# The router's matmuls on bf16 parts: eight small matmuls per tile of tokens in place of four in fp32r

## What is computed

```python
x = x + tanh(g_xattn[0]) * attention(layernorm(x), ctx, Wq, Wk, Wv, Wo, q_norm_w, k_norm_w, ...)
y = layernorm(x)
probs = softmax(y @ w_router, axis=-1)          # w_router: 256 x 8
top_v, top_i = top_k(probs, 2)
top_v = top_v / sum(top_v)
# two of eight experts per token, weighted by top_v, and a shared expert
x = x + tanh(g_ffn[0]) * (2.5 * routed + shared)
```

## Time and profile before

| | us |
|---|---|
| median of 3 runs (1231.79 to 1233.23) | 1233.18 |
| the profiled execution | 1232.97 |
| its span, first to last instruction | 1231.2 |
| granted TensorE clock, mean of the span | 0.998 of full speed |

### The profile page before, as it was taken

The page is one execution under the profiler, slowest core; times in us unless marked ns, Lnnn a source line. Parts: engine busy times, 40 slices in busy tenths (PEclk is TensorE's granted clock), DMA queues, the critical chain, the costliest instruction groups (busy, mean ns, idle before and its releaser), DMA issues.

```text
span 1231.2 us, 31490 instructions
## 1 busy us (share of the span) xinstructions
PE 1206.6 (98%) x8781; PEld 1137.8 (92%) x8782; DVE 1009.8 (82%) x2992; ACT 884.6 (72%) x3754; POOL 922.4 (75%) x1124
## 2 busy tenths in 40 slices
PE   6899999999999999999999999999999999999998
PEld 3788999999999999999999999999999899999997
DVE  8788888888888888888888888888888677777443
ACT  7978777777777777777777777777777546666322
POOL 2778888888888888888888888888887425555654
PEclk9999999999999999999999999999999999999999
DMA  6634233322222222223333333222236536554574
GB/s 179 198 116 130 73 109 104 100 90 90 90 90 90 94 90 94 90 90 96 115 107 98 103 108 118 90 75 75 75 110 214 191 108 185 168 156 148 187 232 155
DMA packets 128792, 148.57 MB, mean 121 GB/s; under 512 B 13824, under 2 KB 108288, under 8 KB 127968
## 3 DMA queue, kind: packets, MB, share of 16 engines
q1 hardware_dynamic: 122256, 130.16, 34.9%
q0 software_dynamic: 6480, 17.77, 3.9%
HBM read 66.93 MB, written 80.76 MB: 120 GB/s over the span
## 4 chain that ended last, share of the span: by engine, by line
PE 92%; DVE 3%; ACT 2%; DMA 1%; issue 1%; SPq 0%; another core or an unknown queue 0%; POOL 0%; DVEq 0%; POOLq 0%; ACTq 0%
PE b_kv L1711 14%; PE b_q L1697 14%; PE b_o L1795 13%; PE b_sc L1769 9%; PE b_aT L1784 9%; PE b_pT L1777 5%; PE b_qT L1758 4%; PE b_q L2031 3%; PE b_kv L2031 3%; PE b_kT L1754 2%; PE b_q L1828 2%; PE b_kT L1828 2%; PE b_aT L1946 1%; PE b_pT L2048 1%; PE b_aT L2048 1%; PE b_o L1747 1%
## 5 line engine op out<-in xcount | busy, mean ns | idle before, releaser
L1711 PE MATMUL b_kv<-w_group,kv_in_hi 128*128 128x256 f32 x992 | 205.6, 305 | 0.0
L957 ACT ACTIVATE probs<-b_sc,neg_max 128x128 f32<-128x128 f32 x512 | 180.0, 371 | 0.1
L747 POOL TENSOR_TENSOR qk_r<-qk_me,minus_half 128x6 f32<-128x6 f32 x128 | 172.2, 1345 | 10.1
L751 POOL TENSOR_TENSOR q_rot<-q_rot,q_sin 128x512 f32<-128x512 f32 x128 | 164.4, 1284 | 6.9 <-DVE q_sin L1273 1.9
L1711 PEld LDWEIGHTS b_kv<-w_group,kv_in_hi 128*128 128x128 f32 x992 | 161.8, 190 | 6.7 <-issue 0.4
L1697 PE MATMUL b_q<-w_group,kv_in_hi 128*128 128x512 f32 x496 | 164.8, 413 | 0.0
L951 ACT ACTIVATE pT<-b_pT 128x512 f32<-128x512 f32 x128 | 76.6, 599 | 99.6 <-PE b_pT L1777 97.5
L1795 PE MATMUL b_o<-wo_hi,aT_hi 128*128 128x256 f32 x480 | 143.5, 299 | 0.1
L1769 PE MATMUL b_sc<-kT,qT 128*128 128x128 f32 x1024 | 135.9, 275 | 6.2 <-ACT qT L946 4.2
L754 POOL TENSOR_TENSOR q_rot<-q_rot,qk_r 128x512 f32<-128x512 f32 x128 | 133.4, 1043 | 10.0
L1711 PE MATMUL b_kv<-w_group,kv_in_lo 128*128 128x256 f32 x496 | 139.6, 282 | 0.0
(11 more groups left out here) (309 smaller groups left out, 3942.2 us busy)
## 6 DMA issues: line engine op xcount, KB each, us to landing
xs_scratch<-zeros SPq DMA_DIRECT2D x34, 1032.0 KB, 6.3
s_in<-xs_scratch SPq DMA_DIRECT2D x71, 129.0 KB
yT_scratch<-yT SPq DMA_DIRECT2D x32, 256.0 KB
yS<-yT_scratch SPq DMA_DIRECT2D x32, 256.0 KB
routed<-ys_scratch SPq DMA_DIRECT2D x32, 256.0 KB, 3.4
w_hi_all<-w_scratch SPq DMA_DIRECT2D x3, 1536.0 KB, 13.2
x_in<-in_x SPq DMA_DIRECT2D x32, 128.0 KB, 2.3
ctx_raw<-in_ctxT SPq DMA_DIRECT2D x32, 128.0 KB, 2.6
```

The lines of the kernel that those rows point to most:

```text
L747: nc.gpsimd.tensor_tensor(qk_r[g % 2][:], qk_me[:], minus_half[:, 0:REP + NB], ALU.pow).then_inc(r_ready, 1)
L751: nc.gpsimd.tensor_tensor(q_rot[g % 2][:], q_rot[g % 2][:], q_sin[g % 2][:], ALU.add) \
L957: last = nc.scalar.activation(probs[:, j, :], b_sc[:, j * P:(j + 1) * P], ACT.Exp, bias=neg_max[g % 2][:, j:j + 1], accum_out=row_sum[g % ...
L1711: last = nc.tensor.matmul(b_kv[:, s * 2 * HD:(s + 1) * 2 * HD], kv_in[p][a][:, c, 2 * s:2 * s + 2, :], wkv_of(b, c)[:, g % KVH, :], start= ...
```

## The change

The tokens' two fp32r parts (high and low) are each written as a bf16 part and the bf16 rest: four bf16 parts. ACT makes the coarse bf16 parts of both in one instruction over 512 columns (`tokens_coarse`), DVE subtracts them in one instruction over 512 columns (`tokens_fine`). The weights are written once, at the start, as three bf16 parts (one ACT instruction, three on DVE that wait for one another, 16 columns wide). The router becomes eight matmuls with a 128 x 24 operand, all bf16, and `copy_logits` adds three parts. On PE the router moves behind `probs_T` and now waits for `y_fine`. Some small tiles are placed elsewhere in memory, and two semaphores become one; the number of events waited for is the same.

```diff
         wr_raw = sb("wr_raw", [P, DC, E], F32)
-        wr_both = sb("wr", [P, DC, 2, E], F32R)
-        wr_s = [wr_both[:, :, a, :] for a in (HI, LO)]
+        wr_bits = sb("wr_bits", [P, DC, 3, E], BF16)
...
+        y_bits = sb("y_bits", [P, 2, 2, DC, P], BF16, late_at)
+        wr_rest = sb("wr_rest", [P, DC, E], F32, late_at)
...
+            def tokens_coarse(t, p):
+
+                need(act, yT_hi, t + 1)
+                need(act, yT_lo, t + 1)
+                need(act, lg_done, t)
+                nc.scalar.activation(y_bits[:, 0, :, :, :].rearrange("p a c n -> p (a c n)"),
+                                     yT_both[p][:].rearrange("p a c n -> p (a c n)").bitcast(F32), ACT.Copy) \
+                  .then_inc(y_coarse, 1)
...
                         normalize_first(n - 1, g - 1)
+                    if g == 3 and not (first and p == 0):
+                        tokens_coarse(t - 1, 1 - p)
...
             tokens_hi(TILES - 1, 1)
+            tokens_coarse(TILES - 1, 1)
             hidden_hi(2)
...
+            def tokens_fine(t, p):
+                need(dve, y_coarse, t + 1)
+                nc.vector.tensor_tensor(y_bits[:, 1, :, :, :].rearrange("p a c n -> p (a c n)"),
+                                        yT_both[p][:].rearrange("p a c n -> p (a c n)").bitcast(F32),
+                                        y_bits[:, 0, :, :, :].rearrange("p a c n -> p (a c n)"), ALU.subtract) \
+                  .then_inc(y_fine, 1)
...
-                nc.vector.tensor_reduce(logits[:], b_kT[:, D:D + 2 * E].rearrange("p (a e) -> p e a", a=2), AX.X,
+                nc.vector.tensor_reduce(logits[:], b_kT[:, D:D + 3 * E].rearrange("p (a e) -> p e a", a=3), AX.X,
                                         ALU.add).then_inc(lg_copied, 1)
...
-                        dve.wait_ge(wr_hi, 1)
-                        nc.vector.tensor_tensor(wr_s[LO][:], wr_raw[:], wr_s[HI][:].bitcast(F32), ALU.subtract) \
-                          .then_inc(wr_lo, 1)
+                        dve.wait_ge(wr_split, 1)
+                        nc.vector.tensor_tensor(wr_rest[:], wr_raw[:], wr_bits[:, :, 0, :], ALU.subtract).then_inc(wr_split, 1)
+                        dve.wait_ge(wr_split, 2)
+                        nc.vector.tensor_copy(wr_bits[:, :, 1, :], wr_rest[:]).then_inc(wr_split, 1)
+                        dve.wait_ge(wr_split, 3)
+                        nc.vector.tensor_tensor(wr_bits[:, :, 2, :], wr_rest[:], wr_bits[:, :, 1, :], ALU.subtract) \
+                          .then_inc(wr_split, 1)
...
                         normalize_y(t - 1, 1 - p)
+                    if g == 3 and not (first and p == 0):
+                        tokens_fine(t - 1, 1 - p)
                     score_max(n, g)
...
             tokens_lo(T1, 1)
+            tokens_fine(T1, 1)
             copy_logits(T1)
...
-                    if g == 3 and not (first and p == 0):
-                        router(t - 1, 1 - p)
                     if g == 1 and not end:
                         normed_x_T(t + 1, 1 - p)
                     if not (first and u < 1):
                         probs_T(n - 1, g - 1)
+                    if g == 3 and not (first and p == 0):
+                        router(t - 1)
...
-                need(pe, yT_lo, t + 1)
-                for c in range(DC):
-                    for a in (HI, LO):
-                        last = nc.tensor.matmul(b_kT[:, D:D + 2 * E], yT[p][a][:, c, :],
-                                                wr_both[:, c, :, :].rearrange("p a e -> p (a e)"),
-                                                start=(c == 0 and a == HI), stop=(c == DC - 1 and a == LO))
+                need(pe, y_fine, t + 1)
+                terms = [(b, a, c) for a in (HI, LO) for b in range(2) for c in range(DC)]
+                for b, a, c in terms:
+                    last = nc.tensor.matmul(b_kT[:, D:D + 3 * E], y_bits[:, b, a, c, :],
+                                            wr_bits[:, c, :, :].rearrange("p a e -> p (a e)"),
+                                            start=((b, a, c) == terms[0]), stop=((b, a, c) == terms[-1]))
                 last.then_inc(lg_done, 1)
```

More of the change, by code:

```diff
@@ L245, in flamingo @@
         top_i = sb("top_i", [P, 8], U32, late_at)
-        top_f = sb("top_f", [P, TOPK], F32, late_at)
-        lead = sb("lead", [P, 1], F32, late_at)
-        lead_t = sb("lead_t", [P, 1], F32, late_at)
-        share = sb("share", [P, TOPK], F32, late_at)
+        few = sb("few", [P, 16], F32, late_at)
+        lead, lead_t = few[:, 0:1], few[:, 1:2]
+        top_f, share, rank, row_f = [few[:, o:o + TOPK] for o in (4, 6, 8, 10)]
         pick = sb("pick", [P, TOPK, E], F32, late_at)
@@ L253, in flamingo @@
         ranked = sb("ranked", [P, TOPK, E], F32, late_at)
-        rank = sb("rank", [P, TOPK], F32, late_at)
-        row_f = sb("row_f", [P, TOPK], F32, late_at)
         row_i = [sb(f"row_i{p}", [P, TOPK], I32, late_at) for p in range(2)]
-        count = sb("count", [P, E], F32, late_at)
-        full = sb("full", [P, E], F32, late_at)
-        upto = sb("upto", [P, E], F32, late_at)
-        worth = sb("worth", [P, E], F32, late_at)
         nowhere = sb("nowhere", [P, MANY], F32, late_at)
-        past, past_w = [sb(n, [P, E], F32, x_res_at) for n in ("past", "past_w")]
+        past, past_w, count, full, upto, worth = [
+            sb(n, [P, E], F32, x_res_at) for n in ("past", "past_w", "count", "full", "upto", "worth")]
         s_first = sb("s_first", [P, 1], F32, x_res_at)
@@ L267, in flamingo @@
         assert x_res_at[0] <= x_res_end
-        slot_table = sb("slot_table", [1, 2, SLOTS], I32, late_at)
-        slot_expert, slot_row = [slot_table[0:1, n, :] for n in range(2)]
+        late_at[0] += 128
         G_WIDE, D_WIDE = DC * GU // G_TILES, DN * D // D_TILES
@@ L275, in flamingo @@
         yS = [[yS_both[r][:, a, :, :] for a in (HI, LO)] for r in range(RING)]
+        slot_table = sb("slot_table", [1, 2, SLOTS], I32, list(late_at))
+        slot_expert, slot_row = [slot_table[0:1, n, :] for n in range(2)]
+        y_bits = sb("y_bits", [P, 2, 2, DC, P], BF16, late_at)
+        wr_rest = sb("wr_rest", [P, DC, E], F32, late_at)
         assert max(late_at[0], hi_at[0]) <= nc.sbuf_usable_end and ring_at[0] <= ring_end, (late_at, ring_at, ring_end)
@@ L1076, in pair @@
                     if first and u == 0:
-                        nc.scalar.activation(wr_s[HI][:], wr_raw[:], ACT.Copy).then_inc(wr_hi, 1)
+                        nc.scalar.activation(wr_bits[:, :, 0, :], wr_raw[:], ACT.Copy).then_inc(wr_split, 1)
                     if g == 3 and not (end or first and p == 0):
@@ L1983, in _ @@
             shared_down(1)
-            router(T1, 1)
+            router(T1)
             shared_hidden_T(2)
```

16 lines of the change are left out of this document (8 added, 8 removed).

## The result

The changed kernel takes **1235.71 us** (median of 9 runs, 1234.94 to 1236.91), the kernel before beside it 1233.05 (9 runs, 1231.79 to 1233.48): a ratio of 1.0021, with a 95% interval of 1.0012 to 1.0030. It is slower by 2.7 us. The forecast was slower by 5.9.

A forecast was written before the change was run, and what follows sets the result against it. PE was taken to bound the kernel, busy 98% of the span. Waits of 11.0 us less a saving of 5.1 gave +5.9 on 1232.97, 1238.9, plus 0.2 to the runs' median: 1239.1 us, range 1229 to 1248.

The forecast's parts named there:

- the lower edge of its own terms: Whole program: the fast end of the forecast by the bounds of its terms alone, 1235.8 to 1243.2 us.
- a saving on PE: PE's router: eight bf16 matmuls at 0.22 us replace 0.38, saving 0.16 a tile, 5.1 us over 32 tiles.
- the size of the waits: PE ahead of the router: idle until `tokens_fine` ends on DVE, 11.0 us summed over all tiles.
- "g" pieces: 16 tiles where DVE comes late behind a piece of this kind: PE waits 0.32 us each, 5.1 in all.
- "d" pieces: 8 tiles with this other kind of piece on DVE: PE waits 0.48 us each, 3.8 in all.
- none: Tiles 26 to 30, without pieces, 5 routers: ACT sets the time, PE waits 0.12 us each, 0.6 in all.
- last tile: Router behind the loop, without cover: PE waits 1.5 us for the ACT and DVE instructions, and its queue waits too.
- The weights' chain at the start: Three weight instructions at the start, 16 columns wide, run once: claimed to cost nothing.
- The wait costs nothing: Ahead of the router: only the saving left, 1228.1 us, or 1229.6 with the last tile's wait; nearly hidden 0.20.
- Costly loads: Router matmuls on PE: each costs its 0.098 us weight load, +18 us, 1257; chance 0.07.
- POOL first: POOL's L751 starts before `tokens_fine`, which waits 1.26 to 1.28 us; 1245.4 if only without pieces; chance 0.08.
- None of it reaches PE: Units with pieces: `score_max` 0.3 to 0.45 us later and L751 some 0.5 later, claimed not to delay PE.

The follow-up runs named there:

- parts_not_read: Changed kernel with the bf16 parts made but unread, the router fp32r again at its old place; ratio 1.0010, 0.9 us over the kernel before.
- old_router_moved: Kernel before with its fp32r router issued behind `probs_T` instead of in front of it; ratio 1.0005, 0.7 us over the kernel before.
- eight_twice: Changed kernel with the eight router matmuls issued twice; ratio 1.0073, 9.3 us over the kernel before, 6.7 over the changed one.
- fine_longer: Changed kernel with a second, unused 160-column subtraction on DVE ahead of `tokens_fine`; ratio 1.0336, 41.6 us over the kernel before.
- router_behind_queries: Changed kernel with the loop's router matmuls issued behind `queries` and `copy_logits` behind `sum_inverse`; ratio 1.0026 against the kernel before.
- wait_in_two: Changed kernel with the four coarse router matmuls first, only the last four waiting for `y_fine`; ratio 1.0003, 0.5 us over the kernel before.
- fine_half: Changed kernel without the fine part of the tokens' low half, 256 columns subtracted and six matmuls; ratio 0.9961, 4.6 us under the kernel before.

## Why the prediction was half right

The forecast was +5.9 us, with 1235.8 us as the lower edge of its own terms; measured were +2.7 and 1235.71.

**What held.** The direction and its cause: a saving on PE against a wait for `tokens_fine`. Eight matmuls at 0.22 were measured at 0.21; ACT's 0.63 at 0.628; DVE's 0.69 at 0.68; next to none of the work on ACT or DVE reached PE by another way (parts_not_read). `exponentials` start 0.42 us behind `queries` (386.55 - 386.13), against 0.77 before (386.13 - 385.36). In units with pieces DVE was ahead of POOL's q sum, as forecast from 0.15 us of distance; in those without it was ahead too, by 0.12 (882.01, 882.13).

**The step that failed is the size of the waits.** Eight tenths of the forecast's 11.0 us were 24 waits whose size was the small difference of two times, and a common term in all of them was too large. The prediction put 0.14 us between DVE's end and the first matmul, 0.07 for the semaphore and 0.07 for a weight load. Measured is 0.06 in all three kinds of wait, and by the records the first load and the first matmul start together (both at 986.08): the load doesn't come on top. And PE was ready 0.05 later than assumed: from the first score matmul to the router without a wait it is 882.80 - 881.47 = 1.33 us, where the prediction had 1.28 from a unit with another small step. Both make every wait shorter, by 0.13 together:

| | forecast wait | measured (`probs_T` to router, less 0.44) | times |
|---|---|---|---|
| "g" pieces | 0.32 | 0.19 | 16 |
| "d" pieces | 0.48 | 0.35 | 8 |
| none | 0.12 | 0 | 5 |
| last tile | 1.5 | 1.30 | 1 |

That is 3.0 + 2.8 + 0 + 1.3 = 7.1 us of waits instead of 11.0 (means over the tiles, with the second tile's 0.34 among the sixteen; for the last tile its idle time). The bounds of the prediction for this term (0.05 to 0.17) did include the measured 0.06; the value taken came from adding two effects of which the row showed one.

**The saving was a little too large.** 0.13 us a tile instead of 0.16, so 4.2 instead of 5.1. The 0.03 is the size of the new place's price, which old_router_moved shows alone. The prediction had counted the matmuls and left the place at nothing.

**Two small terms were missed.** The weights' chain at the start, set at nothing, costs 0.3: three small DVE instructions, each 0.2 behind the last, stand ahead of `q_rot`, and PE waits 0.22 for `q_sin` at 66.16. In the last units of the attention a wait of PE for POOL's `k_rot` (0.6 in the kernel before) is gone, 0.3 net of what PE waits there instead. Together: 7.1 - 4.2 + 0.3 - 0.3 = 2.9, against PE's delay of 2.7 at 1003 us; the rest lies in hundredths of a microsecond between the routers.

**The rivals.** "The wait costs nothing" was wrong for the tiles with pieces and right for the five without. "Costly loads" was refuted by eight_twice. "POOL first" didn't happen in any tile, but fine_longer shows how near it was: 0.23 us later on DVE, and each tile costs 1.3 more. That it stayed out is luck in part, in the units without pieces above all, where the forecast had the two engines within 0.1 us. The prediction gave for POOL winning in the 24 tiles with pieces 1.28 each; measured is 1.07, beside the 0.23 of the added work.

**A reading that was missing.** "None of it reaches PE" holds as long as PE keeps about the pace of before; where the wait ahead of the router was taken out and the unit fell to 7.34 us (router_behind_queries), DVE's row reached PE in the next unit. The prediction judged DVE by what it had left on average and by the wait it caused. The busy time of DVE in the unit g = 3 alone, 6.44 of 7.46 us, would have shown that 0.68 more leaves it little room (7.12), even before POOL's 0.3 on top.

## What to carry to other kernels

When an edit gives the bounding engine less work but hangs it on a new chain through another engine, read that other engine's busy time in the very unit in which the chain runs: if it is nearly full there, a wait that is moved can come back elsewhere (router_behind_queries). What paid here was to let less of PE's work wait (wait_in_two, 2.2 us) and to shorten that engine's instruction (fine_half: 0.27 us less of DVE's time a tile and two matmuls less turned +2.7 us into -4.6, at the price of precision). Where a wait is the difference of two near times that recurs in every tile, measure the common term (end of one engine to start of the next) on a row without other effects, since an error of 0.08 us counts 24 times. And look at who is next to DVE in the queue for SBUF: an instruction issued 0.08 us too late cost 1.07 us in each tile, most of POOL's 1.27 (fine_longer).
